# Softmax sums of an attention loop: a third adding transfer a group, one block of products with ones, and the sums inverted 16 a partition

## The reference

```
q = (query @ Wq).reshape(b, sq, NUM_HEADS, HEAD_DIM).transpose(0, 2, 1, 3)
k = (key @ Wk).reshape(b, sk, NUM_KV_HEADS, HEAD_DIM).transpose(0, 2, 1, 3)
v = (value @ Wv).reshape(b, sk, NUM_KV_HEADS, HEAD_DIM).transpose(0, 2, 1, 3)
k = jnp.repeat(k, rep, axis=1)
v = jnp.repeat(v, rep, axis=1)
scores = jnp.einsum('bhqd,bhkd->bhqk', q, k) * scale
probs = jax.nn.softmax(scores, axis=-1)
out = jnp.einsum('bhqk,bhkd->bhqd', probs, v)
out = out.transpose(0, 2, 1, 3).reshape(b, sq, DIM)
return out @ Wo
```

## Time and profile before

| | |
|---|---|
| median of 3 runs | 1245.8 us (1245.58 to 1246.04) |
| profiled execution | 1244.74 us, its span 1242.9 us |
| TensorE busy | 1209.7 us, 97% of the span |
| VectorE busy | 830.0 us, 67% |
| GpSimd busy | 686.0 us, 55% |
| ScalarE busy | 475.4 us, 38% |
| TensorE's granted clock, mean | 0.997 of full speed |

### The profile page before, as it was taken

How to read it: one execution, slowest core, us unless ns; L and a number is a source line. 1 busy time by engine, 2 the same in 40 slices (tenths; PEclk the granted TensorE clock), 3 DMA queues, 4 the chain that set the end, 5 groups by cost and what they waited for, 6 DMA issues and landing times.

```text
span 1242.9 us, 16721 instructions
## 1 busy us (share of the span) xinstructions
PE 1209.7 (97%) x6358; PEld 509.0 (41%) x6440; DVE 830.0 (67%) x1419; ACT 475.4 (38%) x826; POOL 686.0 (55%) x300
## 2 busy tenths in 40 slices
PE   8997899999999999999999999999999999999998
PEld 6663444444444322222222222234444444444443
DVE  7999831433456788998899898435559846737622
ACT  4675321000100476776777677743252010010000
POOL 6006998500081288888989889870075553525510
PEclk9998999999999999999999999999999999999999
DMA  9577143311461054544545444443374443523301
GB/s 354 172 252 188 52 121 117 85 35 35 86 188 62 27 117 112 108 102 96 114 106 117 92 105 105 81 90 60 93 220 137 135 136 102 172 82 102 118 17 51
DMA packets 86764, 141.20 MB, mean 114 GB/s; under 512 B 49056, under 2 KB 59296, under 8 KB 82592
## 3 DMA queue, kind: packets, MB, share of 16 engines
q1 hardware_dynamic: 52176, 95.60, 24.8%
q0 software_dynamic: 4608, 33.56, 13.4%
q10 hardware_dynamic: 29904, 11.02, 4.0%
HBM read 85.49 MB, written 10.49 MB: 77 GB/s over the span
## 4 chain that ended last, share of the span: by engine, by line
PE 76%; DVE 16%; issue 2%; DMA 2%; POOL 2%; ACT 1%; SPq 0%; DVEq 0%; POOLq 0%; ACTq 0%
PE bank L660 46%; PE bank L910 9%; DVE mxp L1691 8%; PE bank L897 7%; PE bank L985 6%; PE bank L942 4%; DVE xn L1681 2%; PE bank L696 2%; PE bank L686 1%; POOL R L648 1%; DVE R L1468 1%; DVE R L1421 1%; POOL R L626 1%; DMA R<-R 1%; DMA XTl<-xn 1%
## 5 line engine op out<-in xcount | busy, mean ns | idle before, releaser
L1691 DVE TENSOR_REDUCE mxp<-bank 128x1 f32<-128x512 f32 x512 | 320.0, 678 | 57.7 <-PE bank L897 57.4
L1322 ACT ACTIVATE R<-bank 128x512 f32<-128x512 f32 x512 | 273.6, 602 | 112.3 <-PE bank L985 111.3
L660 PE MATMUL bank<-XTh,R 128*128 128x512 bf16 x878 | 273.8, 379 | 3.6 <-POOL R L648 1.5
L626 POOL TENSOR_TENSOR R<-R 128x2048 f32<-128x2048 f32 x48 | 218.7, 4556 | 82.7 <-ACT R L1322 76.3
L660 PE MATMUL bank<-R 128*128 128x512 bf16 x941 | 208.0, 379 | 1.1
L660 PE MATMUL bank<-XTl,R 128*128 128x512 bf16 x436 | 165.2, 379 | 0.6
L648 POOL TENSOR_TENSOR R<-stage_pair,R 128x1024 bf16<-128x1024 f32 x32 | 76.0, 2389 | 130.1 <-DVE R L1849 69.4
L660 PEld LDWEIGHTS bank<-R 128*128 128x128 bf16 x960 | 93.9, 98 | 113.3
L897 PE MATMUL bank<-R 96*128 96x512 bf16 x352 | 134.7, 383 | 3.1 <-DVE mxp L1691 3.0
L910 PE MATMUL bank<-R,stage_c 128*32 128x512 f32 x1024 | 136.4, 604 | 0.7 <-ACT R L1322 0.7
L985 PE MATMUL bank<-R 98*128 98x512 bf16 x352 | 134.0, 381 | 1.2 <-DVE R L1719 0.8
(11 more groups left out here) (193 smaller groups left out, 1503.7 us busy)
## 6 DMA issues: line engine op xcount, KB each, us to landing
stage_pair<-wts_in SPq DMA_DIRECT2D x35, 512.0 KB, 3.6
R<-R POOLq DMA_DIRECT2D x16, 1024.0 KB, 7.0
stage_pair<-R POOLq DMA_DIRECT2D x16, 1024.0 KB, 7.0
stage_pair<-w_in SPq DMA_DIRECT2D x32, 512.0 KB, 3.5
stage_c<-w_in SPq DMA_DIRECT2D x32, 512.0 KB, 3.6
R<-q_scr SPq DMA_DIRECT2D x48, 128.0 KB, 2.5
XTh<-ctx_t_in SPq DMA_DIRECT2D x11, 512.0 KB, 7.4
XTh<-ctx_nat_in SPq DMA_DIRECT2D x9, 512.0 KB, 4.1
```

What stands on the lines that cost most here:

```text
L626: pool.tensor_tensor(PS[(0, 1, 2, 1)[j]], PB[2 * j % 4], PB[2 * j % 4 + 1], ALU.add).then_inc(p_add, 1)
L660: mm = pe.matmul(o, a, m, start=first and a is ah and bs is bh, stop=last and a is al)
L1322: act.activation(PB[kt % 4][:, h * S:(h + 1) * S], bank[t_bank(g, t)][:, :], ACT.Exp, scale=float(HD) ** -0.5).then_inc(exp_done, 1)
L1691: dve.tensor_reduce(mxp[head // REP % 2][:, m, n // 2, n % 2:n % 2 + 1], bank[s_bank(u)][:, :], AX.X, ALU.max).then_inc(s_max, 1)
```

## The change

The totals are now made whole before TensorE sees them. After the second pair, a transfer adds its sum onto the total (the first pair's); before the fourth pair, one adds the third pair's; and after the first add of the next group, a third one adds the fourth pair's. TensorE then multiplies one total a group with ones, at step 30 of the next group (TOTAL_AT = 30). Only the last group keeps two blocks: there the fourth pair's sum is added onto the third's and both it and the total are multiplied.

Since a total now lives longer, it alternates: for even groups it is the first half of R4, for odd groups a part of XTh that is free in the first half of the loop (xth_1: in each partition eight runs of 256 float32, 1 KB each), and from group 8 on a part of V that is no longer needed. The two other buffers, the second half of R4 and stage_pair, change places each group (beside).

For groups 0 to 13 (FEW_GROUPS), the sums are inverted in another layout: SP sends the four rows of sums to a tile few of 128 x 16 (16 sums a partition), VectorE inverts that in one instruction at step 8, and SP writes it to DRAM (r_scr) and reads it back with four broadcasts to 32 partitions each. The last two groups are inverted as before. ScalarE copies the sums at step 31 instead of 20.

```
 T_BANKS = (2, 3, 4)
-TOTAL_AT = (2, 18)
-SUM_OUT_AT = 20
+TOTAL_AT = 30
+SUM_OUT_AT = 31
+FEW_AT = 8
+FEW = REP * S // P
+FEW_GROUPS = GROUPS - 2
...
+        few = sb("few", [P, 2 * FEW], F32)
...
+        xth_1 = per_tile(XTh[:, :].bitcast(F32))[:, :, B * S // 4:B * S // 2]
...
+        def total_in(g):
+
+            if g % 2 == 0:
+                return pieces(PS[0])
+            return xth_1 if g < KV_HEADS else pieces(V[:, 0:REP * S])
+
+        def beside(g, i):
+
+            return pieces(PS[1 + (g + i) % 2])
...
+            def sums_in(g):
+
+                sp.wait_ge(sum_out, g + 1)
+                for h in range(REP):
+                    sp.dma_start(few[h * HD:(h + 1) * HD, 0:FEW],
+                                 p_sum[h * HD:h * HD + 1, :].rearrange("o (i n) -> o i n", n=FEW)).then_inc(few_in, 16)
+
+            def reciprocals_in(g):
+
+                sp.wait_ge(few_rec, g + 1)
+                if g > 0:
+                    sp.wait_ge(rec_in, 16 * REP * g)
+                    sp.wait_ge(o_mul, g)
+                sp.dma_start(r_scr.rearrange("h (i n) -> (h i) n", n=FEW), few[:, FEW:2 * FEW]).then_inc(few_out, 16)
+                sp.wait_ge(few_out, 16 * (g + 1))
+                for h in range(REP):
+                    sp.dma_start(rec[h * HD:(h + 1) * HD, :], r_scr[h:h + 1, :].to_broadcast([HD, S])).then_inc(rec_in, 16)
...
             for g in range(1, GROUPS):
                 rows_in(g)
+                if g >= 2:
+                    sums_in(g - 2)
                 if g + 2 < GROUPS:
                     sp.wait_ge(st_mm, STEPS * g)
                     queries_in(g + 2)
                     keys_in(g + 2)
+                if g >= 2:
+                    reciprocals_in(g - 2)
...
+            def add_pair(g, j):
+
+                pool.wait_ge(exp_done, STEPS * g + 2 * REP * (j + 1))
+                if j == 0:
+                    if g >= 2:
+                        pool.wait_ge(one_mm, g - 1)
+                    dst = total_in(g)
+                elif j == 1:
+                    if g > 0:
+                        pool.wait_ge(ps_c, 16 * g)
+                    dst = beside(g, 0)
+                elif j == 2:
+                    if g > 0:
+                        pool.wait_ge(ps_d, 16 * g)
+                    dst = beside(g, 1)
+                else:
+                    pool.wait_ge(ps_b, 16 * (g + 1))
+                    dst = beside(g, 0)
+                pool.tensor_tensor(dst, pieces(PB[2 * j % 4]), pieces(PB[2 * j % 4 + 1]), ALU.add).then_inc(p_add, 1)
+
             for g in range(GROUPS):
                 for j in range(KT // 2):
-                    pool.wait_ge(exp_done, STEPS * g + 2 * REP * (j + 1))
                     if j == 3:
-                        pool.wait_ge(ps_sum[0], 16 * (g + 1))
-                    elif g > 0 and j == 1:
-                        pool.wait_ge(ps_sum[1], 16 * g)
-                    elif g > 0:
-                        pool.wait_ge(one_mm, 2 * (g - 1) + j // 2 + 1)
-                    pool.tensor_tensor(PS[(0, 1, 2, 1)[j]], PB[2 * j % 4], PB[2 * j % 4 + 1], ALU.add).then_inc(p_add, 1)
-                    if j % 2 == 1:
-                        pool.wait_ge(p_add, 4 * g + j + 1)
-                        pool.dma_start(PS[j - 1], PS[1], accum_op=ALU.add).then_inc(ps_sum[j // 2], 16)
+                        pool.wait_ge(p_add, 4 * g + 3)
+                        pool.wait_ge(ps_b, 16 * (g + 1))
+                        if g + 1 < GROUPS:
+                            pool.dma_start(total_in(g), beside(g, 1), accum_op=ALU.add).then_inc(ps_c, 16)
+                    add_pair(g, j)
+                    if j == 0 and g > 0:
+                        pool.wait_ge(p_add, 4 * g)
+                        pool.wait_ge(ps_c, 16 * g)
+                        pool.dma_start(total_in(g - 1), beside(g - 1, 0), accum_op=ALU.add).then_inc(ps_d, 16)
+                    if j == 1:
+                        pool.wait_ge(p_add, 4 * g + 2)
+                        pool.dma_start(total_in(g), beside(g, 0), accum_op=ALU.add).then_inc(ps_b, 16)
...
-            def total(g, j):
-
-                pe.wait_ge(ps_sum[j], 16 * (g + 1))
-                if j == 0 and g > 0:
+            def total(g):
+
+                if g > 0:
                     pe.wait_ge(sum_out, g)
-                over_keys(bank[6], onesf[:, 0:HD], PS[2 * j], j == 0, j == 1).then_inc(one_mm, 1)
+                if g + 1 < GROUPS:
+                    pe.wait_ge(ps_d, 16 * (g + 1))
+                    over_pieces(onesf[:, 0:HD], total_in(g), True, True).then_inc(one_mm, 1)
...
+            def invert_few(g):
+                dve.wait_ge(few_in, 16 * REP * (g + 1))
+                if g > 0:
+                    dve.wait_ge(few_out, 16 * g)
+                dve.reciprocal(few[:, FEW:2 * FEW], few[:, 0:FEW]).then_inc(few_rec, 1)
...
-                    if g > 1 and t < STEPS // 2 and t % 4 == 2:
-                        invert(g - 2, t // 4)
+                    if g > 1 and t == FEW_AT:
+                        invert_few(g - 2)
```

More of the change, by code:

```diff
@@ L298, in build @@
         p_add = sem("p_add")
-        ps_sum = [sem(f"ps_sum{i}") for i in range(2)]
+        ps_b = sem("ps_b")
+        ps_c = sem("ps_c")
+        ps_d = sem("ps_d")
         one_mm = sem("one_mm")
@@ L912, in over_keys, with over_pieces @@
                 return mm
+            def over_pieces(weights, probs, first, last):
+                n = KT // REP
+                for h in range(REP):
+                    mm = pe.matmul(bank[6][h * HD:(h + 1) * HD, :].rearrange("p (k n) -> p k n", k=n), weights,
+                                   probs[:, h * n:(h + 1) * n, :], start=first, stop=last)
+                return mm
             def weigh(g, kt):
```

40 lines of the change are left out of this document (29 added, 11 removed).

## The result

| | before | after |
|---|---|---|
| median of 4 runs | 1245.69 us (1244.81 to 1246.04) | 1301.88 us (1299.89 to 1304.96) |
| ratio after / before | | 1.0456, 95% interval 1.0443 to 1.0468 |
| span of the profiled execution | 1242.9 us | 1301.3 us |
| mean granted clock of TensorE | 0.997 | 0.967 |
| turn of the row maxima in step 16, first to last of 15 | 431.24 to 786.84 | 431.27 to 844.92 |

The changed kernel is 56 us slower where I had forecast 13 us faster. All of it lies in the attention loop: the first turn comes at the same time, the last one 58.1 us later, and what follows it takes 456 us in both. A group took 25.6 us; now the twelve in the middle take 28.0 to 32.0, 30.4 in the mean.

The account below looks back on a forecast made before the run. The loop was taken as bound by TensorE, and for half of each of 12 groups by VectorE just above it. 1244.7 - 12.9 - 12.0 + 9.2 + 2.4 = 1231.4, forecast as 1232.5 us, range 1219 to 1262.

Parts of the forecast that it names:

- SP's queue: At a group's start, query and key loads go behind the sums' copies: 0.2 us a group, +2.4, bounds 0 to 18.
- Before, the two never overlap: SP's loads and GpSimd's adding transfer in the kernel before: the transfer issued at 588.19 lands before the loads at 595.49.
- Queries and keys come late: Rival: all loads wait behind the adding transfer, 18 us instead of 2.4; 1248 us, or 1239 with pieces free; chance 0.11.
- One block less: TensorE in groups 0 to 14: one block of products with ones less, 0.86 us each, 12.9 us gained.
- Reciprocals: VectorE in groups 2 to 13: 16 a partition instead of 512 saves 1.0 us a group, 12.0 us.
- 1 KB pieces: GpSimd's issues into XTh, groups 1, 3, 5, 7: 1.0 us longer for 1024 pieces, +9.2 us, bounds 0 to 70.
- The pieces are dear: Rival: GpSimd's issues into XTh eat the gain at 2.1 us extra; at 3.5 the time is 1262; chance 0.24.
- gap of 7.98 us before the fourth add: GpSimd, second add's issue to the point before the fourth: longer than the 7.0 us landing, so landings priced 0.
- issues into XTh over 3 us: Sign of a wrong direction: GpSimd's issues this long make pairs of groups up to group 8 take over 55 us.
- GpSimd at 23.4 of 23.8, and the landings: Loop: GpSimd's 23.39 us fit TensorE's 23.76, 0.37 spare; landings cost 0, up to 1 us a group.
- Landings bind in every group: Rival: waits before the third and fourth add cost 6 to 12 us more, 1239 to 1245 us; chance 0.12.
- The end: Last group: two transfers in sequence and both blocks stay, so the end keeps its length, 0 us.

Follow-up runs that it names:

- filler: The changed kernel with sixteen spare products ahead of TensorE's wait for the keys in step 12 of each group: 1281.56 us, ratio 1.0291.
- adding_only: The changed kernel with VectorE's old reciprocals and SP's old order, keeping the three adding transfers and one block of ones: 1249.94 us, ratio 1.0045.
- few_only: The kernel before with only the reciprocals of 16 a partition added, sums copied at step 20: 1242.36 us, ratio 0.9977.
- few_four: few_only with a fourth buffer, in XTh and then V, for each group's fourth pair: 1236.54 us, ratio 0.9934.
- no_second: The changed kernel without the adding transfer of the third pair's sum, 1 added to the copied sums: 1227.81 us, ratio 0.9857.
- clear: The changed kernel with the third pair's transfer issued behind the fourth add, loads ahead of the sums' copies, reciprocal at step 12: 1284.41 us.
- late_three: The changed kernel with scores 48 steps ahead, reciprocal at step 12, division behind third add, lower part behind fourth, upper part at step 31: 1252.7 us.
- few_late: few_only with the sums copied at step 31 instead of 20: 1241.7 us, ratio 0.9974 to the kernel before.

## Why the prediction was wrong

*SP's queue (+2.4, bounds 0 to 18): the step that failed.* The overlap was seen: the loads "now run beside the transfer that GpSimd issues at 1.1 to 1.7 us of the group". But each of the ten issues was priced at 0.4 to 0.6 us and the last load's landing at 2.1, from rows in which no adding transfer runs, and the upper bound only let the loads end about 1 us after C. What was mis-sized is above all the issuing. Measured, the last keys were issued 8.3 us after the first copy instead of 4.6; their landing took 1.9 to 2.4 us in 7 groups, as priced, and 3.5 to 6.7 in 6. The wait was 3.3 us a group against 0.2 (bound 1.5). That alone is 43 us. Issuing and landing beside another transfer were unknown costs, and their bounds should have been as wide as for the 1 KB pieces. The prediction's "Before, the two never overlap" is a misreading as well: 13 of the loads in the kernel before were issued 6 to 9 us after an adding transfer that had not yet landed, and landed in 2.4 us in the mean. They met it only at its end.

*Left out: the clock.* No term and no bound said what TensorE's clock does behind a wait. With 78.5 us at half clock it added some 31 us to the 43; `filler` got 20 us back.

*Queries and keys come late (rival, 0.11).* Close to the mechanism, at 1248 us instead of 1302, and with too low a chance; but what waited behind the transfer was SP's issuing more than the loads' pieces. The Trainium skill ("DMA: Bandwidth & Descriptors", Queues, rings and completion order), cited there, says that an engine takes turns between its queues packet by packet; the direction agrees with the traces (keys 2.1 us alone, 5.2 in the groups where all three lie beside an adding transfer). I did not let the rule widen the bound, and that was the mistake of judgement.

*One block less (-12.9): right.* A group of adding_only at its best takes 24.79 us instead of 25.62, 0.83 less where 0.86 was forecast.

*Reciprocals (-12.0): right in kind, not seen in full.* VectorE's pieces in the loop have left the chain. Alone they brought 2.8 us (few_only), for want of a buffer, and 8.3 with one (few_four). With C away the terms can be read together: `no_second` took 1227.8 us, 17.3 less than the 1245.1 beside it, where the forecast said 13 and 22.5 without the pieces' cost; its steady groups take 23.91 us where the forecast said 23.76. It does one transfer less, though, than the kernel that was forecast.

*1 KB pieces (+9.2): the issue was about right, 0.7 against 1.0; the landing was left out.* GpSimd's issues of C, by form (issue ns min/median/max, first and last start):

```profile
L694 POOL DMA_DIRECT2D R<-stage_pair x8: 871/971/1105, 444.5 to 860.1; - x8
L694 POOL DMA_DIRECT2D XTh<-R x4: 1552/1563/1567, 470.7 to 653.2; - x4
```

The rival "The pieces are dear" had the right side for a wrong reason: its break-even of 2.1 us extra is three times what was measured. What the pieces also cost is their landing, which the forecast put at 7.0 us, at most 8.5, for all transfers: into XTh it takes 8.9 to 10.6, longer than the gap of 7.98 us before the fourth add. In adding_only the first eight groups take 26.2 us where the best take 24.8, some 11 us in all, and GpSimd waits 9.4 us in 6 for transfers into XTh; that this is near the 9.2 forecast is luck. The Trainium skill ("DMA: Bandwidth & Descriptors", Anatomy of one DMA) lets one emit many descriptors before the cost shows up; here 1024 pieces instead of 128 cost 0.7 us, so the measurement decides against reading it as free. The rule of the prediction that issues into XTh over 3 us would turn the sign was, then, a test of the wrong cause.

*GpSimd at 23.4 of 23.8, and the landings.* In the changed kernel GpSimd waited only 13.2 us in 8 for its own transfers, and ScalarE 14.6 in 7 for GpSimd's adds. The margin is as thin as the forecast said: in adding_only, clear and late_three ScalarE waits 16 to 64 us for adds. "Landings bind in every group" goes too far even for these: adding_only has groups of 24.8 us. In the changed kernel TensorE's wait gave GpSimd time.

*The end: 0.* Right, 456.1 us before and 456.4 after.

What stays open is why SP issues more slowly beside an adding transfer; the runs show that it does, and no run here tells the cause.

## What to carry to other kernels

A small DMA's duration holds only for the traffic it was measured in: before adding a large transfer, list what is issued and what must land within its 7 to 9 us. Here, what was issued in its first 4 us took about 6 us to land instead of 2, and ten small transfers queued one behind another took 1.6 times as long to issue; what met only its last 2 us was hardly slowed. Where a consumer has less slack than that, give it slack or move the large transfer; removing the work in front of TensorE gains nothing if TensorE then waits. A wait of TensorE costs more than its length: here waits of 43 us brought some 31 us more, since the clock was halved behind them.

## What the runs showed of the hardware

- Ten small transfers of SP issued one after another: 8.3 us from the first issue to the last beside an adding transfer of 1 MB, 5.1 in few_late, where at most the end of one lies beside them.
- Small transfers issued 1 to 4 us after such a transfer landed in 5.9 us in the mean, those issued 7 us after it or later in 2.3, and alone in 1.7 to 2.5.
- An adding transfer in 1 KB pieces lands in 9.2 us in the median, at most 10.6, where 8 KB pieces take 7.7 in the same kernel; its issue takes 1.56 us against 0.87.
- In the changed kernel, idle times of 2.4 to 4.9 us were followed by TensorE at the 1.2 GHz level, each stretch 3.4 or 6.8 us long and in 11 of 12 cases begun before the idle time ended; one of 1.2 us was not. With spare products in their place it stayed at 2.4 GHz throughout the loop.
